# Stage one of a fused attention and expert kernel: turns in pairs over two PSUM banks, copies shared anew, own engine orders

## The reference

```python
x = x + tanh(g_xattn[0]) * L0_xattn_ref(ctx_1024, layernorm(x), mask, ...)
# in it, for each of 32 batches: latents are 256 rows of x, the context 120 rows
q = ln @ w_q                                    # 8 heads of 64
kv_in = concatenate([xn, ln], axis=1)           # 120 + 256 = 376 rows
k, v = split(kv_in @ w_kv, 2, axis=-1)
sim = einsum('bhid,bhjd->bhij', q * scale, k);  sim = where(mask, sim, -max)
out = einsum('bhij,bhjd->bhid', softmax(sim), v)
return layer_norm(out @ w_out, g_o, b_o)
x = x + tanh(g_ffn[0]) * L0_ffn_ref(layernorm(x), ...)   # top 2 of 8 experts, by batch, 40 rows each at most
```

## Time and profile before

| | us |
|---|---|
| median of 3 runs (2328.33 to 2338.77) | 2334.22 |
| the profiled execution | 2332.35 |
| its span | 2330.2 |
| TensorE matmuls, busy in the span | 2229.5 (96%) |
| TensorE weight loads, beside them | 1867.0 (80%) |
| VectorE | 1767.9 (76%) |
| ScalarE | 1287.4 (55%) |
| GpSimd | 659.9 (28%) |

### The profile page before, as it was taken

The page is one execution under the profiler, slowest core; times in us unless marked ns, Lnnn a source line. Parts: engine busy times, 40 slices in busy tenths (PEclk is TensorE's granted clock), DMA queues, the critical chain, the costliest instruction groups (busy, mean ns, idle before and its releaser), DMA issues. The chain is left out here.

```text
span 2330.2 us, 52907 instructions
## 1 busy us (share of the span) xinstructions
PE 2229.5 (96%) x15232; PEld 1867.0 (80%) x15232; DVE 1767.9 (76%) x6078; ACT 1287.4 (55%) x3250; POOL 659.9 (28%) x1162
## 2 busy tenths in 40 slices
PE   6999999999999999999899999999899999999998
PEld 5777777777677777777699999999788888888887
DVE  5888878788777887788865555555588888888897
ACT  5776666666666766667543333333354444454444
POOL 1123222232232322322210000001355555555542
PEclk9999999999999999999999999999999999999999
DMA  6220010110100100001042222222122111221110
GB/s 212 87 92 29 27 38 26 29 36 19 37 27 28 37 26 29 30 27 32 15 142 77 81 83 83 82 64 74 55 57 61 54 57 51 60 60 60 58 44 19
DMA packets 111557, 128.34 MB, mean 55 GB/s; under 512 B 14898, under 2 KB 98089, under 8 KB 111264
## 3 DMA queue, kind: packets, MB, share of 16 engines
q1 hardware_dynamic: 98249, 105.06, 14.2%
q0 software_dynamic: 12288, 21.21, 3.2%
q10 hardware_dynamic: 855, 0.19, 0.1%
HBM read 84.26 MB, written 54.53 MB: 60 GB/s over the span
## 5 line engine op out<-in xcount | busy, mean ns | idle before, releaser
L709 ACT ACTIVATE a_prob<-a_prob,a_nmax 128x376 f32<-128x376 f32 x512 | 307.1, 604 | 26.8 <-DVE a_nmax L855 26.0
L1116 PEld LDWEIGHTS a_turned<-keep_ident,a_prob 128*128 128x128 f32 (+1 forms) x1536 | 173.6, 139 | 160.0 <-issue 118.0
L1116 PE MATMUL a_turned<-keep_ident,a_prob 128*128 128x128 f32 (+1 forms) x1536 | 265.1, 281 | 31.3 <-DVE a_probT L874 27.1
L1420 ACT ACTIVATE e_hidden<-e_first,keep_b 128x256 f32<-128x256 f32 x320 | 134.4, 472 | 286.8 <-PE e_first L80 285.4
L855 DVE CUSTOM_DVE_ANT_0 a_prob<-a_score,a_mask_row 128x376 f32<-128x376 f32 x512 | 262.5, 541 | 19.9 <-DVE r_lg L257 9.7
L717 ACT ACTIVATE a_probT<-a_turned 128x384 f32<-128x384 f32 x256 | 125.9, 492 | 241.9 <-PE a_turned L1116 236.4
L80 PE MATMUL e_second<-e_w,e_hidden 128*128 128x256 f32 x1920 | 239.5, 284 | 0.0
L80 PEld LDWEIGHTS e_second<-e_w,e_hidden 128*128 128x128 f32 x1920 | 232.6, 192 | 0.0
L874 DVE COPY a_probT<-a_turned 128x384 f32<-128x384 f32 x256 | 141.3, 552 | 119.4 <-PE a_turned L1116 61.2
L171 POOL TENSOR_SCALAR r_var<-r_mv 128x2 f32<-128x2 f32 x64 | 12.3, 192 | 686.1 <-DVE r_mv L889 520.7
L867 DVE TENSOR_SCALAR a_prob<-a_prob,a_rden 128x376 f32<-128x376 f32 x512 | 201.3, 419 | 2.2
(11 more groups left out here) (212 smaller groups left out, 5114.6 us busy)
## 6 DMA issues: line engine op xcount, KB each, us to landing
w_in<-W SPq DMA_DIRECT2D x32, 512.0 KB
slots<-a_zeros SPq DMA_DIRECT2D x8, 1280.0 KB, 9.1
keep_rows<-slots SPq DMA_DIRECT2D x40, 256.0 KB, 3.8
answers<-e_y SPq DMA_DIRECT2D x40, 256.0 KB, 2.2
a_xn<-x SPq DMA_DIRECT2D x32, 256.0 KB, 3.6
a_xr<-x SPq DMA_DIRECT2D x32, 256.0 KB, 2.8
x<-r_x SPq DMA_DIRECT2D x32, 256.0 KB, 2.7
w_in<-x SPq DMA_DIRECT2D x32, 256.0 KB, 2.8
```

What stands on the lines that cost most here:

```text
L709: nc.scalar.activation(prob[:, u % 4, a], prob[:, u % 4, a], ACT.Exp, bias=nmax[:, u % 4, a:a + 1], scale=-1.0, accum_out=den[:, u % 4, a: ...
L1116: last = nc.tensor.transpose(turned[0:hi - lo, j * P:(j + 1) * P], prob[:, u % 4, a, lo:hi], ident[:])
L1420: nc.scalar.activation(hidden[:, 2 * j + i], first[:, j, i * CH:(i + 1) * CH], ACT.Relu, bias=b1[:, 2 * j + i, bass.ds(e, 1)]).then_inc(re ...
```

## The change

- There are two banks `turned[0]` and `turned[1]`, one for each head. `turn_prob(b, u)` turns both heads of a tile in one go: it waits for both normalised heads and for the copies of both heads of the tile before, then issues six transposes.
- The bank for this is gained by making `work[1]` and `values` one bank. `times_v` now writes `work[0]`; the router's products and the turned context lie in `work[1]`.
- Of head 1's eight copies a batch, ScalarE makes those of u = 0, 2, 4 and 6, VectorE keeps u = 1, 3, 5 and 7. Head 0 stays with ScalarE.
- TensorE, VectorE and ScalarE have new orders within a step, and waits fit for them. `choose` and `router_exp` move from the end of a step into the next one. On GpSimd `norm1` comes behind `norm0`.

The core of the diff:

```diff
-        turned = pb("a_turned", [P, 512])
-        work = [pb(f"a_work{i}", [P, 512]) for i in range(2)]
+        turned = [pb(f"a_turned{i}", [P, 512]) for i in range(2)]
+        work = [pb("a_work0", [P, 512]), values]
...
-            def turn_prob(b, u, a):
-
-                eng.wait_ge(norm_ok[a], NG * b + u + 1)
-                at_least(eng, prob_ok[1 - a], NG * b + u + a)
-                for j, lo, hi in VALUE_ROWS:
-                    last = nc.tensor.transpose(turned[0:hi - lo, j * P:(j + 1) * P], prob[:, u % 4, a, lo:hi],
-                                               ident[:])
-                last.then_inc(turned_ok[a], 1)
+            def turn_prob(b, u):
+
+                for a in range(2):
+                    eng.wait_ge(norm_ok[a], NG * b + u + 1)
+                    at_least(eng, prob_ok[a], NG * b + u)
+                for a in range(2):
+                    for j, lo, hi in VALUE_ROWS:
+                        last = nc.tensor.transpose(turned[a][0:hi - lo, j * P:(j + 1) * P], prob[:, u % 4, a, lo:hi],
+                                                   ident[:])
+                    last.then_inc(turned_ok[a], 1)
...
 def project_v(b, p, j):
                 if j == 2:
+                    eng.wait_ge(kvin_lo, 2 * (b + 1))
                     eng.wait_ge(q_hi, 2 * b + 2)
-                    eng.wait_ge(kvin_lo, 2 * (b + 1))
-                elif j == 1:
-                    eng.wait_ge(v_ok, 3 * b + 1)
+                    at_least(eng, rT_out, b - 1)
+                elif j == 0:
+                    eng.wait_ge(k_hi, KI * b + 4)
+                    at_least(eng, att_lo, KI * b)
+                elif isinstance(b, int) and b == B - 1:
+                    eng.wait_ge(soft, N_SOFT * (b - 2) + 1)
                 else:
-                    eng.wait_ge(k_hi, KI * b + 4)
+                    eng.wait_ge(kvc_ok, KD * (b + 2))
...
 def times_v(b, p, m):
-                elif m == 1:
-                    eng.wait_ge(att_lo, KI * b + 1)
...
+                elif isinstance(b, int) and b == B - 1:
+                    eng.wait_ge(att_lo, KI * b + m)
                 else:
-                    eng.wait_ge(att_lo, KI * b + 3)
...
+                    eng.wait_ge(k_hi, KI * (b + 1) + m + 1)
                 for j, lo, hi in VALUE_ROWS:
                     for a in range(2):
-                        last = nc.tensor.matmul(values[64 * a:64 * a + 64, 0:S], vo[0:hi - lo, p, j, m, a],
+                        last = nc.tensor.matmul(work[0][64 * a:64 * a + 64, 0:S], vo[0:hi - lo, p, j, m, a],
```

VectorE's new order at the head of a step (mask line, `stat` and more in front of `att_low` 3) and at its end:

```diff
+                if live(s - 2):
+                    normalise(s - 2, 1, 0)
+                if live(s - 1) and not (isinstance(s, int) and s == 1):
+                    kvin_low(s - 1, q, 0)
                 if live(s - 1):
                     mask_line(s - 1, q)
-                if live(s - 2):
+                if live(s):
+                    stat(s, p)
+                if live(s - 2):
+                    over_sum(s - 2, 2)
+                    row_max(s - 2, p, 4, 0)
+                    row_max(s - 2, p, 4, 1)
                     normalise(s - 2, 2, 1)
                 if live(s - 3):
                     att_low(s - 3, 3)
...
+                if here(s - 4):
+                    choose(eng, s - 4)
...
                 if here(s - 3):
                     logits_in(eng, s - 3)
...
+                if live(s - 1):
+                    normalise(s - 1, 1, 1)
+                if live(s - 2):
+                    turned_out(s - 2, 7, 1)
+                if live(s - 1):
+                    row_max(s - 1, q, 3, 1)
+                    row_max(s - 1, q, 3, 0)
                 if here(s - 3):
                     logits_shift(eng, s - 3)
```

More of the change, by code:

```diff
@@ L341, in router_logits @@
         eng.wait_ge(rT_out, b + 1)
+        if not (isinstance(b, int) and b >= B - 2):
+            eng.wait_ge(v_ok, 3 * (b + 2) + 1)
         for i in range(QT):
@@ L476, in attend @@
         LAST = 3
-        turned_keys = turned[:, 0:3 * P].rearrange("p (j q) -> p j q", j=3)
+        turned_keys = [bank[:, 0:3 * P].rearrange("p (j q) -> p j q", j=3) for bank in turned]
         def live(b, last=B):
@@ L621, in step @@
                     eng.wait_ge(zeroed, 16 * N_CLEAR)
-                if here(s - 3):
-                    norm1(eng, s - 3)
                 if live(s):
@@ L626, in step @@
                 if here(s - 3):
+                    norm1(eng, s - 3)
                     norm2(eng, s - 3)
@@ L737, in step @@
                 if live(s - 2):
-                    k_high(s - 2, p, 3)
+                    turned_out(s - 2, 0, 0)
+                if here(s - 4):
+                    router_exp(eng, s - 4)
+                if live(s - 1):
+                    affine_c(s - 1)
+                    kvin_high(s - 1, q, 1)
                 if live(s - 3):
@@ L905, in weights_lower @@
                     .then_inc(w_low, 1)
-            nc.vector.memset(turned[:], 0.0).then_inc(const_ok, 1)
+            for bank in turned:
+                nc.vector.memset(bank[:], 0.0).then_inc(const_ok, 1)
             nc.vector.memset(mask_row[:, :, C:NKV], 0.0).then_inc(const_ok, 1)
@@ L933, in step @@
                     w1_lower(1)
+                if here(s - 4):
+                    choose(eng, s - 4)
                 if live(s - 2):
-                    row_max(s - 2, p, 4, 1)
-                    row_max(s - 2, p, 4, 0)
+                    turned_out(s - 2, 1, 1)
+                    over_sum(s - 2, 3)
+                    row_max(s - 2, p, 5, 1)
                     row_max(s - 2, p, 5, 0)
                     normalise(s - 2, 2, 0)
-                if live(s):
-                    stat(s, p)
-                if live(s - 2):
-                    turned_out(s - 2, 1, 1)
-                    row_max(s - 2, p, 5, 1)
-                    over_sum(s - 2, 3)
-                if live(s - 1) and not (isinstance(s, int) and s == 1):
-                    kvin_low(s - 1, q, 0)
-                    kvin_low(s - 1, q, 1)
+                    normalise(s - 2, 3, 1)
+                    over_sum(s - 2, 4)
+                    normalise(s - 2, 3, 0)
                 if live(s - 3):
                     out_stat(s - 3)
-                if live(s - 2):
-                    over_sum(s - 2, 4)
-                if routed(s - 4):
-                    counts_in(eng, s - 4)
+                if live(s - 1) and not (isinstance(s, int) and s == 1):
+                    kvin_low(s - 1, q, 1)
                 if live(s - 3):
@@ L970, in step @@
                 if live(s - 2):
-                    att_low(s - 2, 0)
-                    turned_out(s - 2, 3, 1)
-                    row_max(s - 2, p, 7, 0)
-                    row_max(s - 2, p, 7, 1)
                     normalise(s - 2, 5, 1)
@@ L1001, in step @@
                 if live(s - 2):
-                    turned_out(s - 2, 6, 1)
-                    normalise(s - 2, 7, 1)
+                    att_low(s - 2, 2)
+                if live(s - 1):
+                    normalise(s - 1, 0, 1)
+                if live(s - 2):
+                    normalise(s - 2, 7, 0)
                 if live(s - 1):
                     normalise(s - 1, 0, 0)
-                    normalise(s - 1, 0, 1)
+                    row_max(s - 1, q, 2, 1)
+                    over_sum(s - 1, 1)
+                    row_max(s - 1, q, 2, 0)
+                if here(s - 3):
+                    logits_in(eng, s - 3)
+                if live(s - 1):
+                    normalise(s - 1, 1, 1)
+                if live(s - 2):
+                    turned_out(s - 2, 7, 1)
+                if live(s - 1):
+                    row_max(s - 1, q, 3, 1)
+                    row_max(s - 1, q, 3, 0)
                 if here(s - 3):
@@ L1037, in turn_x @@
                 eng.wait_ge(xh_ok, 3 * (b + 1))
-                at_least(eng, k_hi, KI * (b - 1) + 3)
+                if isinstance(b, int) and b == 1:
+                    eng.wait_ge(k_hi, 3)
+                at_least(eng, att_lo, KI * (b - 2) + 3)
                 for k in range(KD):
@@ L1046, in turn_c @@
                 eng.wait_ge(xh_ok, 3 * (b + 1))
-                at_least(eng, att_lo, KI * (b - 2) + 3)
+                at_least(eng, v_ok, 3 * (b - 1) + 1)
+                at_least(eng, soft, N_SOFT * (b - 3) + 1)
                 for k in range(KD):
-                    last = nc.tensor.transpose(values[:, k * C:(k + 1) * C],
+                    last = nc.tensor.transpose(work[1][:, k * C:(k + 1) * C],
                                                xh[0:C, 2, k * P:(k + 1) * P], ident[0:C, 0:C])
@@ L1170, in step @@
                     scores(s - 2, p, 5)
-                    turn_prob(s - 2, 1, 0)
+                if live(s - 3):
+                    times_v(s - 3, q, 3)
+                if live(s - 2):
+                    turn_prob(s - 2, 1)
+                    project_v(s - 2, p, 1)
                     project_v(s - 2, p, 0)
-                    turn_prob(s - 2, 1, 1)
```

252 lines of the change are left out of this document (103 added, 149 removed).

## The result

| | before | after |
|---|---|---|
| median of 4 executions each, on one chip | 2335.24 | 2361.36 |
| the profiled execution, span | 2330.2 | 2360.5 |
| sum of the 27 full steps from the fifth on | 965.1 | 989.9 |
| the 16 without a loop jump, mean | 35.2 | 35.1 |
| the 11 with a jump, mean | 36.6 | 39.0 |

The change makes the kernel slower: ratio 1.0111, interval 1.0082 to 1.0141. Two later jobs, on two different chips, repeat it with 1.010 and 1.012. The forecast was 2310, and the time lies outside its range.

The account below looks back on a forecast made before the run. TensorE's queue was taken as the bound. Plain steps 25, jump steps 1 and ends 3 made 29 us, less 5 allowed for x: 24 saved, 2310 from 2334. Range 2289 to 2345; the forecast's own, 2300 to 2320.

Parts of the forecast that it names:

- The bound and the stalls of before: TensorE's queue bounds the old kernel: plain step 34.1 us stream plus 1.19 stall; steps with a loop jump 36.5.
- Pairs: TensorE's turns of both heads together: 5.2 us for 5.7 in singles; 0.4 a step taken as saved.
- rival 4: Pairs cost what singles cost: stream stays 34.1, 11 us more, 2321; chance 0.12.
- The copies: Four of VectorE's copies a batch go to ScalarE; both engines stay under TensorE, so their price is hidden.
- The middle of the step: Between head and end of TensorE's new order: free of stalls, with 0.5 to 3 us of slack.
- The late report: VectorE's copy starting 2.26 us after its turn's shown end; near that work 1 to 2 us slack, taken as absorbed.
- rival 2: The late report stalls another turn by the same 1.2 us in plain steps: 2329, no change; chance 0.17.
- The head of the step: project_v 0 waits for VectorE's att_low 3, done at 4.9 and wanted at 4.95: no stall, no reserve.
- x: How much later than the layout VectorE reaches att_low 3; 0.2 us a step allowed, 5 us over 27 steps.
- rival 1: VectorE comes late to att_low 3, so project_v 0 waits; 2345 at 1.5 us a step, 2359 at 2; chance 0.18.
- The jump: After a loop jump VectorE starts at 3.25; stalls of 0.8 and 1.9 make the step 36.4, as long as now.
- The ends: Outside the 27 full steps: 2 us saved at stage one's end, 1 in its first full steps; 3 together.

Follow-up runs that it names:

- a_vcopies2: The changed kernel with all of head 1's copies on VectorE again; 2355.48, ratio 1.012 to before.
- a_mix2: The changed kernel with VectorE's att_low 3 moved behind kvin_low and ahead of mask line, stat and two normalises; 2329.90, ratio 1.001 to before.
- a_attlow: The changed kernel with VectorE's att_low 3 moved ahead of kvin_low, mask line, stat and the second normalise; 2345.12, ratio 1.007 to before.

## Why the prediction was wrong

In short: the pairs saved nearly nothing of TensorE's stream, the late report was not absorbed but met times_v 2 in all 27 full steps, and behind a jump more work stood between VectorE's gap and what TensorE waits for, with a low clock on top. The steps of the working, one by one:

*The bound and the stalls of before:* right. 34.1 of stream plus 1.2 of late report is a plain step; without the scatters it takes 34.07. A long step is 2.2 us more in that kernel too. What the prediction did not see is that in before's long steps the same copy is only 1.0 late, which stalls nothing: without the scatters they take 36.3 for 36.6.

*Pairs:* this step failed in size (rival 4's mechanism held). Groups from start to start in an unstalled step: 16 singles sum to 5.7, as said; 8 pairs to 5.57, not 5.2:

```profile
706.47 0.82 PE L1131 MATMUL a_turned<-keep_ident,a_prob 128*128 128x128 f32 x6
707.04 1.67 PE L80 MATMUL keep_bank<-a_kvin,a_wq 128*128 128x256 f32 x12
...
710.09 0.87 PE L1131 MATMUL a_turned<-keep_ident,a_prob 128*128 128x128 f32 x6
710.89 1.53 PE L1121 MATMUL a_score<-a_kT,a_qT 64*128 64x376 f32 x8
```

The 0.57 before a projection is as forecast, but the pairs before scores cost 0.75 to 0.80 and those before the turn of c and project_v 1 0.69 and 0.63. The stream is 34.05, against 34.07 in before: nothing to be seen was saved, where 0.4 was forecast. Price: 0.35 x 27 = 9 us.

*The copies:* right, hidden, and by a_vcopies2 worth nothing.

*The middle of the step:* right except for one place, below. No other wait on a shared bank appears there.

*The late report:* this is the step that failed. "In my layout what stands near the same work ... has 1 to 2 us of slack, ... so I take it as absorbed" put the term at nothing. The slack had been looked for at the turns alone, and the layout has no entry for times_v 2 and the router's turn between turn 6 (24.6) and scores 2 and 3 (28.3). The next writer of project_k 2's own bank is times_v 2, 2.3 us behind project_k 2's start without a stall (1.14 for the project, 0.43 for the router's turn, 0.75 for the pair). Of these the product takes 1.30 by its modelled end and ScalarE's copy 0.48: a slack of 0.5 against a report 1.46 late. It costs 1.0 in each of the 27 steps, 26 to 27 us: rival 2's mechanism at times_v instead of a turn, and in the long steps too. What the prediction took from the Trainium skill (Perfetto Trace Analysis, "Summary: the profiler window per engine type"), that a TensorE end is an estimate and the way of its semaphore isn't shown, fits: the lateness met ScalarE's copy as it had met VectorE's, and moving copies did not remove it.

*The head of the step:* tight, but whole in plain steps. project_v 0 starts 1.48 behind project_v 1 in them, so x was about 0, not 0.2 (5 us kept for nothing), and rival 1 did not come in plain steps. Behind a jump its mechanism is what costs: VectorE comes late to att_low 3, as the prediction's own walk had it.

*The jump:* the walk was good and the sum was not. Stalls of 0.8 and 1.9 were forecast, 1.0 and 2.0 measured, and VectorE starts 3.30 into the step above, for a forecast of 3.25. But "as long as now (36.5)" rested on 33.7 as the base. By terms: 34.05 + 1.0 (late report) + 3.0 (stalls) = 38.05, and 37.9 is measured; then 1.6 to 1.8 more in 7 of the 11 for the low clock, which the sum had no term for. Over 11 steps: 26.6 us lost where 1 was to be won. a_mix2 shows that it need not be: with project_v 0's wait out of the gap's reach the long steps are 36.5 and all at a clock of 1.00, late report included. The same wait stands in the third step (36.2 for 34.1), where there is no jump and VectorE is held up by another wait; there too a_mix2 has 34.2.

*The ends:* -3 forecast, +5.5 in these two executions, and that is mostly chance. From the last turn of x to the first turn of expert rows it takes 75.2 us in before and 78.6 in the changed kernel, which has a clock of 0.64 over the 19 us shown above, where `times_v` takes 2.83 and `output` 5.46 for 1.52 and 3.07. But before's second execution runs that stretch at half clock too, and takes 84.1 for it:

```profile
1150.00:1170.00 20.00, 16.12 (x67) 9.59 (x66) 9.76 (x37) 7.43 (x17) 5.27 (x5) 0.50 0.02 7
```

In five of the six profiled executions of the old order this stretch has a mean clock of 0.84 to 0.95 and takes 78.8 to 84.1 us, in eight of the twelve of the new order 76.1 to 79.2 at 0.89 to 0.96. Where the clock is 1.00 it is 75.2 in the old order (one) and 73.3 to 73.6 in the new one (four), so the shorter chain did win about the 2 us that it should. On the chip of both repetitions the changed kernel is 12.8 us *shorter* behind the last full step, and still 24.6 slower by its median. What the change costs in the medians, 24.6 to 26.8 us, is about what its 27 full steps lose (24.8 in the first two executions).

*Together,* for the two profiled executions, as an estimate: late report 27, pairs 9, longer stalls at the jump 2, low clock 12, ends 8.5, less the 5 that were kept for x, make 54; the forecast span was 2306, and 2360.5 came.

*Range and chances:* the terms that went wrong had a rival each, but for the low clock and the ends, and the rivals were priced one at a time. Rivals 2 and 4 together, in 27 steps, already give 2310 + 27 + 9 = 2346, at the upper end (2345). The late report deserved the better part of the chance: nothing in the trace said that it would be shorter, only that another instruction would meet it. The prediction's own sign of being wrong came too: plain steps did not fall under 35.

## What to carry to other kernels

A delay that comes with other work in the same stretch of time (here the scatters), and not with one instruction, need not go away when its victim is moved: find every next user of each result that lies in that stretch, the next writer of its bank too, and give the slack of each. At a loop jump ask which engine stalls and put in its first instructions only what no other engine waits for within 3 us, or write the loop out: that alone made the kernel before 1.5 to 1.6% faster, which is the best complete version run here. In steps without either stall the two orders take the same: 34.05 to 34.07 and 34.07 to 34.10. A stall on TensorE can cost more than its length, since the clock may be lower behind it.

## What was not expected of the hardware

- What waits for TensorE's work starts 0.6 to 2.3 us behind its modelled end beside the scatters, and 0.04 behind it in both orders when the four scatters a batch are taken out. How late it is differs with the code (2.2 in most plain steps against 0.7 on one chip, same scatters, loop or none), with the step (2.2 in before's plain steps, 1.0 in its long ones) and with the chip or the occasion (0.04 in all three kernels with scatters on the chip where before took 2304, against 0.6 to 2.3 on the others). Each of the four jobs had its own chip, so chip and occasion can't be told apart. Why is open; it was not tried to move the scatters.
- VectorE stands for 2.6 to 3.4 us at each of the 11 jumps; TensorE shows no wait of its own there. With the loop written out no such gap is left in the full steps. The Trainium skill (Runtime: NRT & Kernel Launch, "Instruction fetch mechanics") says that a taken branch whose target lies outside the prefetched window stalls until that page is fetched. VectorE's gaps at the jumps agree with it; no run here shows where the window ends.
- Behind stalls of 1.0 and 2.0 us TensorE ran partly at the lower level, in 7, 8 and 7 of 11 cases in the three executions of the changed kernel and in 4 of 11 without the scatters. With the one stall of up to 1.0 (a_attlow, a_mix2) it never did, but neither did it in a_vcopies2, where two waits of up to 1.5 and 1.8 stand at the same place: all 11 long steps there have a clock of 1.00. Its third step has waits of 0.6 and 1.9 and a clock of 1.00, and the same kernel in the other job, with the same waits, has 0.96 there. So the length of the stalls alone does not decide it, and what does is open.
